# In the experts' groups VectorE adds the diagonal's masks while it takes the row maxima, in place of PE's mask products

## The reference

```
scores = einsum('bhnd,bhmd->bhnm', Q, K) * scale
scores = where(causal, scores, -inf)
attn = softmax(scores)
out = einsum('bhnm,bhmd->bhnd', attn, V)
```

## Time and profile before

| | |
|---|---|
| time, median of 3 runs | 999.36 us (999.10 to 1001.29) |
| profiled execution, span | 1022.0 us (the page gives no other time of it) |
| PE busy | 907.5 us, 89% of the span |
| VectorE busy | 847.0 us, 83% |
| ScalarE busy | 728.5 us, 71% |
| GpSimd busy | 462.9 us, 45% |
| the reduces at L1275 | 576, 641.4 us |
| the mask products at L1421 | 1024, 103.6 us by their own spans |
| group 2 to group 5 (kind `experts`) | 361.2 to 792.6 us |

### The profile page before, as it was taken

One profiled execution on the slowest core, in us unless ns is written; L12 is line 12 of the kernel. 1 busy time (PEld: TensorE's weight loads), 2 busy tenths in 40 slices (PEclk: granted clock), 3 DMA queues, 4 the chain that ended last, 5 costly groups with the idle time before them and its releaser, 6 DMA issues. The chain is left out here.

```text
span 1022.0 us, 22104 instructions
## 1 busy us (share of the span) xinstructions
PE 907.5 (89%) x7874; PEld 392.7 (38%) x7874; DVE 847.0 (83%) x1096; ACT 728.5 (71%) x1542; POOL 462.9 (45%) x588
## 2 busy tenths in 40 slices
PE   2888446999999999999999899999999999999888
PEld 1554311332432334344434444344434333322257
DVE  6999789899899878886889688877888799894846
ACT  3556200788788878787888788778878788789822
POOL 4677568565201253344833474354132245355610
PEclk8999755999999999999999999999999999999979
DMA  9766810301200324244413542255334321112113
GB/s 324 267 248 248 276 46 11 105 3 38 68 2 2 115 78 121 76 133 147 125 53 98 151 143 74 72 162 132 77 85 125 90 62 49 32 58 64 37 52 124
DMA packets 82084, 106.65 MB, mean 104 GB/s; under 512 B 10000, under 2 KB 59064, under 8 KB 80952
## 3 DMA queue, kind: packets, MB, share of 16 engines
q1 hardware_dynamic: 74488, 85.83, 26.1%
q0 software_dynamic: 6528, 17.83, 6.8%
q10 hardware_dynamic: 960, 1.57, 0.5%
HBM read 67.37 MB, written 37.50 MB: 103 GB/s over the span
## 5 line engine op out<-in xcount | busy, mean ns | idle before, releaser
L1275 DVE TENSOR_REDUCE blk<-psP 128x2 f32<-128x1024 f32 (+2 forms) x576 | 641.4, 1162 | 103.5 <-PE psP L1421 53.7
L1221 ACT ACTIVATE probs<-psS 128x512 f32<-128x512 f32 (+3 forms) x1280 | 589.2, 541 | 162.2 <-PE psS L1458 153.1
L1458 PE MATMUL psS<-Qs,Ks 50*128 50x512 f16 (+3 forms) x1280 | 332.0, 353 | 24.5 <-ACT probs L1221 15.4
L1418 PE MATMUL psP<-Ks,Qs 48*128 48x512 f16 (+3 forms) x1280 | 299.6, 363 | 31.7 <-DVE blk L1275 20.5
L1514 PE MATMUL psO<-probs,Vs 128*32 128x512 f32 (+3 forms) x2560 | 300.3, 547 | 6.0 <-POOL probs L1124 4.9
L1124 POOL TENSOR_SCALAR_AFFINE_SELECT probs<-probs 128x512 f32<-128x512 f32 x128 | 88.1, 689 | 356.3 <-ACT probs L1221 317.4
L1458 PEld LDWEIGHTS psS<-Qs,Ks 50*128 50x128 f16 x1280 | 96.4, 93 | 256.6 <-ACT probs L1221 149.2
L1418 PEld LDWEIGHTS psP<-Ks,Qs 48*128 48x128 f16 x1280 | 80.4, 94 | 132.9 <-DVE blk L1275 94.8
L1421 PE MATMUL psP<-later,eye 64*128 64x128 bf16 x1024 | 103.6, 223 | 0.0
L1514 PEld LDWEIGHTS psO<-probs,Vs 128*32 128x32 f32 x2560 | 52.9, 108 | 86.4 <-issue 65.2
L1421 PEld LDWEIGHTS psP<-later,eye 64*128 64x128 bf16 x1024 | 78.1, 98 | 19.6 <-issue 1.7
(11 more groups left out here) (170 smaller groups left out, 729.3 us busy)
## 6 DMA issues: line engine op xcount, KB each, us to landing
xn<-we_scratch SPq DMA_DIRECT2D x72, 256.0 KB
expert_scratch<-xn SPq DMA_DIRECT2D x36, 256.0 KB
v_scratch<-vst SPq DMA_DIRECT2D x8, 1024.0 KB, 4.0
qk_scratch<-part SPq DMA_DIRECT2D x32, 256.0 KB, 4.0
Vs<-v_scratch SPq DMA_DIRECT2D x16, 512.0 KB, 3.9
Qs<-qk_scratch SPq DMA_DIRECT2D x168, 32.0 KB
Ks<-qk_scratch SPq DMA_DIRECT2D x168, 32.0 KB
acc<-x SPq DMA_DIRECT2D x8, 512.0 KB, 9.2
```

The lines of the kernel that those rows point to most:

```text
L1221: nc.scalar.activation(probs[u % NPR][:, h, q0:CH], psS[:, k % SB, q0:CH], ACT.Exp, scale=exp_scale).then_inc(s_read[k % SB], 1)
L1275: nc.vector.tensor_reduce(out, src, AX.X, ALU.max).then_inc(item_ok[slot], 1)
L1418: ins = pe.matmul(psP[:, slot, at:at + w], Qs[r][rows, qt // CT, p, t * P:(t + 1) * P], Ks[r][rows, kc, p, 0:w], start=True, stop=True)
L1458: pe.matmul(psS[:, k % SB, q0:CH], Ks[r][rows, kt // CT, p, kt % CT * P:(kt % CT + 1) * P], Qs[r][rows, c, p, q0:CH], start=True, stop=Tru ...
```

## The change

VectorE gets another way to read a diagonal item, `reduce_hidden`: for each head one `tensor_tensor_reduce` that adds a table of masks (`hide`, float32: zeros, and -3e38 in its last 128 columns where the key is later than the query) to the scores in PSUM, writes the sums as bfloat16 to a buffer that nobody reads (`shown`), and writes their maximum to the head's column of `blk`. It is used in the groups of kind `experts` alone, and there PE leaves out the two mask products of each head. The first items and the other four groups work as before. GpSimd makes `hide` once, behind its first 64 tables, and VectorE waits for it ahead of each such item (`hide_ok`). PE's written orders stay as they are.

```diff
--- before.py
+++ after.py
@@ -809,6 +809,8 @@
 
         bt = [flat[:, 10 * CH + i * D:10 * CH + (i + 1) * D] for i in range(2)]
         one3 = sb("one3", [P, P], BF16)
+        hide = flat[:, 13 * CH:14 * CH]
+        shown = [flat[:, (14 + i) * CH:(15 + i) * CH].bitcast(BF16) for i in range(2)]
         probs = [sb(f"probs{i}", [P, HG, CH]) for i in range(NPR)]
         ones = sb("ones", [P, CH], F16)
         MQ = HG * CT
@@ -867,6 +869,8 @@
         bt_ok = sem("bt_ok")
         ones_ok = sem("ones_ok")
         added = sem("added")
+        hide_step = sem("hide_step")
+        hide_ok = sem("hide_ok")
 
         WALK = (3, 2, 0, 1)
         FREED = {2: 1, 1: 0}
@@ -981,6 +985,7 @@
         KINDS = ("plain", "route", "experts", "behind", "last")
         orders = {kind: order_of(kind) for kind in KINDS}
         KIND = ["plain", "route"] + ["experts"] * 4 + ["behind", "last"]
+        HIDING = ("experts",)
 
 
 
@@ -1164,6 +1169,10 @@
 
             for n in range(TILES):
                 tables(n)
+            nc.gpsimd.memset(hide[:, :], 0.0).then_inc(hide_step, 1)
+            pool.wait_ge(hide_step, ONE + 1)
+            nc.gpsimd.affine_select(out=hide[:, CH - P:CH], in_=hide[:, CH - P:CH], compare_op=ALU.is_ge, fill=LOW, base=0,
+                                    pattern=[[-1, P]], channel_multiplier=1).then_inc(hide_ok, 1)
             for g in range(GROUPS):
                 if g == 2:
                     split(0)
@@ -1274,6 +1283,19 @@
                     src = psP[:, slot, :].rearrange("p (a q n) -> p (a q) n", a=SIDES, q=PAIRS)[:, :, 0:w]
                 nc.vector.tensor_reduce(out, src, AX.X, ALU.max).then_inc(item_ok[slot], 1)
 
+            def reduce_hidden(item, slot):
+
+                qt, p0, np_, kc, w = item[2:7]
+                for a in range(SIDES):
+                    for p in range(p0, p0 + np_):
+                        n = a * np_ + p - p0
+                        row = qt // CT * MQ + (a * PAIRS + p) * CT + qt % CT
+                        at = a * CH + (p - p0) * (CH // np_)
+                        ins = nc.vector.tensor_tensor_reduce(out=shown[slot][:, n * w:(n + 1) * w], in0=psP[:, slot, at:at + w],
+                                                             in1=hide[:, CH - w:CH], scale=1.0, scalar=LOW, op0=ALU.add,
+                                                             op1=ALU.max, accum_out=blk[:, row, kc:kc + 1])
+                ins.then_inc(item_ok[slot], 1)
+
             def turned(slot, turn):
                 nc.vector.tensor_copy(nmT[turn % 2][:, :], psP[0:MROWS, slot, :].bitcast(F16)[:, 0:P]).then_inc(item_ok[slot], 1)
 
@@ -1380,7 +1402,11 @@
                     if item[0] == "r":
                         list_rows(item[1], slot, uses(g, n))
                     elif item[0] == "q":
-                        reduce(item, slot)
+                        if kind in HIDING and item[7]:
+                            dve.wait_ge(hide_ok, ONE + 1)
+                            reduce_hidden(item, slot)
+                        else:
+                            reduce(item, slot)
                         key = (item[1], item[2] // CT)
                         if not any(x[0] == "q" and (x[1], x[2] // CT) == key for x in items[n + 1:]):
                             lasts = [max(k for k in range(n + 1) if items[k][0] == "q" and slot_of(k) == s)
@@ -1409,7 +1435,7 @@
             def sides(rows):
                 return [slice(a * ROW0, a * ROW0 + rows) for a in range(SIDES)]
 
-            def scores_q(item, a, slot, r):
+            def scores_q(item, a, slot, r, hiding=False):
 
                 qt, p0, np_, kc, w, last = item[2:8]
                 t, rows, all_rows = qt % CT, slice(a * ROW0, a * ROW0 + PR), slice(a * ROW0, (a + 1) * ROW0)
@@ -1417,7 +1443,7 @@
                     at = a * CH + (p - p0) * (CH // np_)
                     ins = pe.matmul(psP[:, slot, at:at + w], Qs[r][rows, qt // CT, p, t * P:(t + 1) * P],
                                     Ks[r][rows, kc, p, 0:w], start=True, stop=True)
-                    for i in range(2 if last else 0):
+                    for i in range(2 if last and not hiding else 0):
                         ins = pe.matmul(psP[:, slot, at + w - P:at + w], eye[all_rows, i, :], later[all_rows, i, :],
                                         start=False, stop=True, skip_group_check=True)
                 ins.then_inc(item_ps[slot], 1)
@@ -1549,7 +1575,7 @@
 
                         pe.wait_ge(item_ok[slot], ONE + uses(g, n))
                         if x[0] == "q":
-                            scores_q(x, x[-1], slot, r ^ x[1])
+                            scores_q(x, x[-1], slot, r ^ x[1], KIND[g] in HIDING)
                         elif x[0] == "m":
                             turn_m(slot, 4 * g + M_TURN[x[1:]])
                         elif x[0] == "r":
```

## The result

The changed kernel takes 1008.73 us, the median of four runs (1005.28 to 1010.80), beside 999.25 us for the kernel before (999.10 to 1001.29): a ratio of 1.0089 [1.0068, 1.0110]. A second set on another occasion gave 1.0101 [1.0057, 1.0144]. One slow execution, of a kernel further down (the whole change, and products of zeros in A), took 1395.76 us at a mean clock of 0.558 and is left out of that kernel's number. The forecast was 1007. The number came out; most of the reasons for it did not.

A forecast was written before the change was run, and what follows sets the result against it. PE was taken to set the pace in experts' groups; 0.9 + 1.3 - 0.2 - 0.2 us over a group's four diagonal stretches gave 7.5 us in four groups, so 999.4 + 7.5 = 1007 us, 8-in-10 range 993 to 1023 us.

The forecast's parts named there:

- A: First of four diagonal stretches of an experts' group; VectorE idle 1.7 us there, PE forecast to be 0.9 us late.
- PE's masks, 11.7 us given back: Mask products dropped from PE in the diagonal stretches: 0.74 us a stretch given back, 11.7 us over the four groups.
- VectorE's fixed cost, 167 ns an instruction: Each new per-head reduce on VectorE costs 77 + 90 ns beyond its elements, making a stretch 2.2 us more.
- The second output's 90 ns: Writing the maximum to blk was taken to add 90 ns to each new VectorE instruction.
- The split's 77 ns: Price per instruction, back to back, of splitting VectorE's diagonal reduces into one for each head.
- My own mark, 0.30 us from start to start at 128 columns: Test set for VectorE: forecast wrong if two new 128-column instructions start far from 0.30 us apart.
- The walk through B, 1.3 us late: Slot-by-slot timeline of B: VectorE's later hand-overs make PE leave it 1.3 us late, its masks already counted.
- B: Second of four diagonal stretches of an experts' group; VectorE idle 1.4 us there, PE's slots tight.
- the free output: Rival: VectorE's second output costs nothing or nearly, 0.8 to 1.3 us a stretch; kernel 3 to 12 us faster; chance 0.23.
- the forecast's 2.2: Extra VectorE time in us for each diagonal stretch: 16 x 0.167 - 6 x 0.077.
- The table on GpSimd: Two mask-table instructions of some 0.6 us each, hidden in 3.98 us of idle time behind the last table.
- All other groups as they were: Expected sign: only experts' groups lengthen, the three whole ones by about 2 us each; the rest keep their times.

The follow-up runs named there:

- the second trace of before: The unchanged kernel before, run and traced once more beside the experiments; 999.57 us, ratio 1.0001, trace span 998.2 us.
- A alone: The change made only in the first diagonal stretch of each experts' group, against the kernel before; 1002.97 us, ratio 1.0036.

## Why the prediction was right in number and wrong in cause

- **PE's masks, 11.7 us given back: wrong.** At full clock two groups without them were 0.15 us shorter and 0.17 us longer. Counting what no other product covers was not far off for PE's own time (its busy time fell by 2.2 us a group, for 2.8 to 3.0), but PE's time was not the group's: it now waits 7.5 us for ScalarE where it waited 3.0. I read 95% busy as "PE sets the pace".
- **VectorE's fixed cost, 167 ns an instruction: the step that failed first.** The second output's 90 ns are 0: the read of the accumulator lies wholly beside the next instruction. The split's 77 ns, the element rate and the durations of the four forms hold. By 16 x 77 - 6 x 77 a stretch is 0.77 us more for VectorE, a group 3.1 us; the windows show 3.2. My own mark, 0.30 us from start to start at 128 columns, reads 0.211.
- **The walk through B, 1.3 us late: wrong with it.** In group 3, at full clock, PE's order is 0.21 us behind the second trace of before when it enters B (37.4 us into the group) and 0.33 us when it leaves (48.1). PE's waits for VectorE are 0.8 us in four groups, not several. What VectorE does cost, 0.25 to 0.6 us a group with PE's masks kept, lies within the free output's 0.8 us a stretch and far under the forecast's 2.2.
- **The rival with the free output had the mechanism of VectorE right and the sign wrong,** for it took PE's 3 us a group as a gain.
- **The clock: put at nothing without a reason.** The granted clock stood in the windows, 0.98 for one group, a fall in A of the kind that the change makes frequent, and I gave it no sentence. That masks which overlap other work can still keep the clock up was in none of my cases. It is some 8 of the 9.5 us: taking the masks out alone loses time (1.0066), and zeros in place of those of A give it back (0.9995).
- **The table on GpSimd: right.** Its two instructions took 0.55 and 0.29 us, with 2.74 us idle behind them.
- **"All other groups as they were": right** (93.2 us for 93.0 behind the experts' groups).

The 7.5 us of the forecast and the 9.5 of the result are near each other by accident: a stall on VectorE too large, a gain on PE too large, and a loss of clock left out.

Open: which groups fall varies between the two traces of the changed kernel, and what decides it was not tried; nor what about the missing products counts, as their number in 5 us does not set the falls apart; nor why the whole change loses more than A alone (1.0036) or than the masks out with plain reduces (1.0045); nor why B fell in two kernels with zeros in A, and not in one that had the masks there. No version here beats the kernel before by what can be measured.

## What to carry to other kernels

Before taking work from TensorE, look at the granted clock beside its busy share, window by window, and don't pass over a single short dip (here one of 3.4 us before the change); products that overlap others and cost no time may be what holds the clock, and the busy share does not show it. A gain on the busiest engine counts only if what it waits for next is earlier too: read that wait, here ScalarE's exponentials, before crediting the busy time. And a result near the forecast proves none of its terms: each needs its own row.

## What the runs showed of the hardware

- VectorE's `tensor_tensor_reduce` with an accumulated maximum is two rows, and the second, 83 ns, starts together with the next instruction: the time from start to start is columns x 1.047 + 77 ns, as for a plain reduce. The Trainium skill, "VectorE: DVE Perf Modes", section "Two Vector instructions with no wait between them", calls it two instructions; the trace agrees on the two rows, and shows that the second adds no time here.
- One PSUM and one SBUF input, both float32, with a bfloat16 output, run at the plain reduce's rate: 687 ns for 512 columns, like the subtraction of the earlier trace rows.
- TensorE's granted clock fell to 1.2 GHz for 3.4 to 6.9 us, after a stretch in which PE was busy for 6.42 of 6.90 us (changed kernel, 362.0 to 368.9). The Trainium skill, "TensorE: Matmul & The Clock Gate", section "HAM oscillation — how this bites in real kernels", tells of such falls behind idle gaps in which PE waits for transfers. No gap of that kind is here, PE's idle time in that stretch being 0.48 us in all; what differed from the kernel before was that 24 of 62 products in 5 us, masks hidden beside others, were gone.
- Products whose results change nothing keep the clock as well: 32 products of zeros a group in place of the masks of A, and no fall in A in the trace (1.00 over 368 to 376 us, for 0.57 in the changed kernel). The same 32 in stretch B left A falling (0.69 over 367 to 378 us).
